# Column maxima of a gated cross-attention: TensorE's eight transposes, or block transposes on VectorE

## The chip, the cores and the metric

One core of one Trainium2 chip. The metric is the device time of one execution in microseconds (us). The engines are named as the profile names them: PE is TensorE's matmul and PEld its weight load, DVE is VectorE, ACT is ScalarE, POOL is GpSimd, SP issues the transfers.

## The reference

Eight independent batches. For each of them, x is 512 x 512 and the memory is 1601 x 256:

```python
memory_proj = einsum('bme,de->bmd', memory, W_mem)
scores = einsum('bnd,bmd->bnm', hidden_states, memory_proj) / sqrt(D)
attn = softmax(scores, axis=-1)
memory_context = einsum('bnm,bmd->bnd', attn, memory_proj)
gate = sigmoid(einsum('bnf,df->bnd', concat([hidden_states, memory_context]), W_gate) + b_gate)
fused = hidden_states + gate * memory_context
out = fused * rsqrt(mean(fused**2, -1) + 1e-6) * norm_w
```

All in fp32. The softmax runs over the 1601 rows of the memory.

## The kernel before

**Arithmetic.** Each fp32 operand of a matmul is split into a rounded high part (`..._hi`, made by ACT) and the rest (`..._lo`, made by DVE, L919), and a product is three matmuls, hi x hi, lo x hi and hi x lo (L387 to L389, L586 to L588). W_mem is moved to the other side: q = W_mem' x, scores = mem q, u = mem' p, and the context and the gate's input are products of u with W_mem and with V, the product of W_mem and the gate's second half.

**Layout.** The scores are held transposed: `s[:, t, :]` has 128 rows of the memory on the partitions (tile t of 13, the last with 65 rows) and the 512 rows of x as columns. A softmax over the memory is then one over partitions and tiles. DVE keeps a running maximum `run` (128 x 512) over the tiles (`running_max`, L931); after the last tile its 128 partitions still have to be reduced to one and the result spread over all partitions, in PSUM bank 3 (`MAX_BANK`), from where `shift` (L960) subtracts it from each tile of s. Before, this is done so: PE transposes the four 128 x 128 blocks of `run` into bank 2 (`transpose_max`, L462), DVE reduces them to `col_max` (128 x 4, L952), and PE transposes `col_max`, each column repeated 128 times, into bank 3 (`spread_max`, L474).

**Stages of a batch b.** 1. Scores: PE makes 13 tiles; ACT copies each to s, DVE takes the running maximum, splits the transposed memory (`mt_lo`) and the memory itself (`mem_lo_part`, pairs of tiles 0 to 6, after ACT's `mem_hi`). 2. PE works on what the batch before has left: the sums of its rows (L489), gate input and context of its four row tiles j (`gate_context`, `context`), while DVE does the maximum. 3. PE makes x times the gate's first half (`gate_x`, L387 to L389 with wg1t). Beside this and stage 4, DVE and ACT run the softmax in 13 steps t: `shift` of tile t+3, ACT's exponential (L755, into `p_tmp`), ACT's `p_hi`, DVE's `p_lo` of tile t; POOL adds the exponentials up (`add_p`, L1229). Among these steps stand the rest of the batch before (`gate_input` L1015, `gate_ctx` L1067, `add_x` L1075), `add_bias` (L986), and DVE's block transposes of the next batch's x and memory (L1025, L1041; a block transpose turns every 32 x 32 block in its place). 4. PE sums u over the tiles (`weighted`); it needs p_lo of each, and after tile 9 it makes q of the next batch (`query`). Then DVE makes `output` (L1084) of the batch before, splits q (`q_lo`), on which the next batch's scores wait, and u (`u_lo`).

**What sets the order.** It is written out by hand: each engine runs its instructions in the order of its own block in the code and waits on semaphores. The first batch, six batches in a loop (1 to 6) and the last one have their own variants. `SPLIT_BY_SCORES` and `SPLIT_BY_SOFTMAX` say at which step the pairs of memory tiles are split, on ACT and on DVE. The eight PSUM banks are shared by the stages.

**The waits that the prediction speaks of:** `weighted(b, t)` on p_lo of t, and for even t on `mem_lo` of its pair; `score(b+1, 0)` on `q_lo`; the last tile on copies by SP that follow p_lo of tile 12 (`stack_last_tile`); in the first batch `gate_x` 2 on `add_bias` 0; in the last batch `tail_gate` on `u_lo`.

Of the kernel before, what the change touches and what calls it, by code (L numbers as in the profile page):

```python
# [36 lines left out]
P = 128  # L37
# [6 lines left out]
def xattn_kernel(nc: bass.Bass, x, mem, w, wg, b_gate, norm_w, out):  # L44
# [19 lines left out]
    with ExitStack() as ctx:  # L64
# [54 lines left out]
        col_max = sb("col_max", [P, NT])  # L119
# [63 lines left out]
        pe_mt, pe_s, pe_max_t, pe_max_rows = sem("pe_mt"), sem("pe_s"), sem("pe_max_t"), sem("pe_max_rows")  # L183
# [42 lines left out]
        SPLIT_BY_SOFTMAX = {5: [6]}  # L226

# [154 lines left out]
        def _(pe):  # L382
# [72 lines left out]
            def transpose_max(b):  # L455


                pe.wait_ge(run_done, (MT - 1) * (b + 1))

                pe.wait_ge(s_copied, MT * (b + 1))  # L460
                for j in range(NT):
                    last = nc.tensor.transpose(  # L462
                        bank[S_BANK][:, j * P : (j + 1) * P], run[:, j * P : (j + 1) * P], ident[:, :])
                last.then_inc(pe_max_t, 1)

            def spread_max(b, first):


                pe.wait_ge(col_max_done, b + 1)
                if not first:  # L470

                    pe.wait_ge(r_done, b)
# [151 lines left out]
            def iteration(b, first, last):  # L624
                scores(b, first)
                if first:
# [6 lines left out]
                    transpose_max(b)  # L633
                    weights(V[0])
                    spread_max(b, first)
# [3 lines left out]
                else:  # L639
                    row_sums(b - 1, True)  # L640
                    gate_context(b - 1, 0)
                    transpose_max(b)
                    context(b - 1, 0)
                    gate_context(b - 1, 1)
                    spread_max(b, first)
# [271 lines left out]
        def _(dve):  # L917
# [28 lines left out]
            def reduce_max(b, first):  # L946
                if not first:

                    dve.wait_ge(pe_max_rows, b)

                dve.wait_ge(pe_max_t, b + 1)
                nc.vector.tensor_reduce(col_max[:, :], bank[S_BANK][:, :].rearrange("p (a n) -> p a n", a=NT),  # L952
                                        AX.X, ALU.max).then_inc(col_max_done, 1)

            def shift(b, t):
                if t == 0:

                    dve.wait_ge(pe_max_rows, b + 1)
# [139 lines left out]
            def iteration(b, first, last):  # L1098
                transpose_mem(b, 2)
                for p in range(MP):  # L1100
# [8 lines left out]
                    for q in SPLIT_BY_SCORES.get(p, []):  # L1109
                        mem_lo_part(b, q)  # L1110
# [18 lines left out]
                else:  # L1129
# [9 lines left out]
                    for t in range(MT):  # L1139
# [5 lines left out]
                        if t in (0, 2, 4):  # L1145
                            gate_ctx(b - 1, 1 + t // 2)
# [148 lines left out]
```

## Time and profile before

| | |
|---|---|
| median of 3 runs | 545.79 us (545.26 to 546.56) |
| the profiled execution | 546.02 us, span 544.0 us |
| granted TensorE clock | 0.998 of full speed |
| PE busy | 533.3 us, 98% |
| PEld busy | 436.6 us, 80% |
| DVE busy | 480.4 us, 88% |
| ACT busy | 315.9 us, 58% |
| POOL busy | 148.0 us, 27% |

The profiled execution takes 2.0 us more than its span, which is what lies around the first and the last instruction. A row of a timeline gives the start and the duration in us; its end is pipelined, so the next instruction of an engine may start some 0.08 us before it. A bracket at the end of a row is idle time ahead of it, with what ended it. The six batches of the loop repeat at a distance of 64.1 us; most rows below are from one of them.

### The profile page before, as it was taken

What the parts mean: (1) busy time and instruction counts of PE and PEld (TensorE: products, weight loads), DVE (VectorE), ACT (ScalarE), POOL (GpSimd) and SP (SyncE); (2) the same over time, 40 slices, a digit from 0 to 9 for tenths busy, and PEclk for the clock granted to TensorE, in tenths of its full rate; (3) what the DMA queues carried; (4) which work ended last, traced back from release to release, by engine and by line L of the source; (5) the groups of instructions that cost most, each with busy time, mean ns of one, the idle gap of its engine ahead of it and who ended that gap; (6) DMA issues with size and microseconds to landing.
All of it is one profiled execution on the core that took longest, in us unless ns stands there. A gap on an engine that the chain in (4) does not pass through costs nothing.

```text
span 544.0 us, 8854 instructions
## 1 busy us (share of the span) xinstructions
PE 533.3 (98%) x2420; PEld 436.6 (80%) x2420; DVE 480.4 (88%) x758; ACT 315.9 (58%) x601; POOL 148.0 (27%) x127
## 2 busy tenths in 40 slices
PE   8899999999999999999999999999999999999994
PEld 7776888888888888888888888888888888888883
DVE  3779958899799997999978998989979999789967
ACT  4575636566465664666465763656556575557523
POOL 0005610065002540036200660015400263004703
PEclk9999999999999999999999999999999999999999
DMA  9855363621576207841278214762068510301033
GB/s 225 262 118 92 96 107 88 113 59 41 141 159 104 93 7 170 175 107 39 85 127 171 76 39 125 161 114 72 25 159 169 120 49 30 125 30 40 1 117 116
DMA packets 185861, 56.37 MB, mean 104 GB/s; under 512 B 161756, under 2 KB 175592, under 8 KB 185844
## 3 DMA queue, kind: packets, MB, share of 16 engines
q1 hardware_dynamic: 185316, 55.64, 43.7%
q10 hardware_dynamic: 528, 0.52, 0.3%
q8 instruction: 8, 0.13, 0.1%
q14 instruction: 9, 0.07, 0.1%
HBM read 46.15 MB, written 8.39 MB: 100 GB/s over the span
## 4 chain that ended last, share of the span: by engine, by line
PE 93%; SPq 3%; DMA 2%; DVE 1%; issue 0%; ACTq 0%; POOLq 0%; POOL 0%; DVEq 0%; ACT 0%
PE bank L387 21%; PE bank L389 21%; PE bank L388 21%; PE bank L586 8%; PE bank L587 8%; PE bank L588 8%; DMA fused<-in_L_xattn_W_gate_dram 2%; SPq L262 2%; PE bank L607 1%; PE bank L489 1%; PE bank L621 1%; PE bank L462 1%; PE bank L474 1%; PE bank L570 1%; DMA x_again<-in_x_dram 1%; PE bank L569 1%
## 5 line engine op out<-in xcount | busy, mean ns | idle before, releaser
L1229 POOL TENSOR_TENSOR psum_rows<-psum_rows,p_tmp 128x512 f32<-128x512 f32 (+1 forms) x88 | 122.9, 1397 | 71.6 <-ACT p_tmp L755 70.0
L919 DVE TENSOR_TENSOR p_lo<-p_tmp,p_hi 128x512 fp32r<-128x512 f32 (+1 forms) x104 | 92.6, 891 | 5.5 <-ACT p_hi L716 5.4
L1229 POOL TENSOR_TENSOR psum_rows<-p_tmp 128x512 f32<-128x512 f32 x8 | 10.4, 1297 | 275.2 <-ACT p_tmp L755 275.2
L755 ACT ACTIVATE p_tmp<-s 128x512 f32<-128x512 f32 (+1 forms) x104 | 64.5, 626 | 30.5 <-DVE s L960 29.3
L387 PE MATMUL bank<-q_hi,mt_hi 128*128 128x512 f32 (+1 forms) x208 | 81.9, 394 | 0.0
L389 PE MATMUL bank<-q_hi,mt_lo 128*128 128x512 f32 (+1 forms) x208 | 81.3, 391 | 0.0
L388 PE MATMUL bank<-q_lo,mt_hi 128*128 128x512 f32 (+1 forms) x208 | 81.2, 390 | 0.0
L586 PE MATMUL bank<-p_hi,mem_hi 128*128 128x512 f32 (+1 forms) x196 | 76.4, 390 | 0.0
L587 PE MATMUL bank<-p_lo,mem_hi 128*128 128x512 f32 (+1 forms) x196 | 76.4, 390 | 0.0
L588 PE MATMUL bank<-p_hi,mem_lo 128*128 128x512 f32 (+1 forms) x196 | 76.3, 390 | 0.0
L716 ACT ACTIVATE s<-bank 128x512 f32<-128x512 f32 (+1 forms) x104 | 62.0, 596 | 19.5 <-PE bank L389 19.1
L960 DVE TENSOR_TENSOR s<-s,bank 128x512 f32<-128x512 f32 (+1 forms) x104 | 68.4, 671 | 0.0
L931 DVE TENSOR_TENSOR run<-run,s 128x512 f32<-128x512 f32 (+1 forms) x88 | 59.9, 681 | 8.1 <-ACT s L716 5.8
L716 ACT ACTIVATE p_hi<-p_tmp 128x512 fp32r<-128x512 f32 (+1 forms) x104 | 63.4, 616 | 0.0
L387 PE MATMUL bank<-wg1t_hi,xt_hi 128*128 128x512 f32 x128 | 50.3, 393 | 0.0
L389 PE MATMUL bank<-wg1t_hi,xt_lo 128*128 128x512 f32 x128 | 49.9, 390 | 0.0
L388 PE MATMUL bank<-wg1t_lo,xt_hi 128*128 128x512 f32 x128 | 49.8, 389 | 0.0
L774 ACT ACTIVATE gate<-gate 128x512 f32<-128x512 f32 x32 | 20.2, 633 | 49.2 <-DVE gate L1015 49.2
L919 DVE TENSOR_TENSOR mt_lo<-bank,mt_hi 128x512 fp32r<-128x512 f32 (+1 forms) x56 | 34.6, 627 | 15.9 <-ACT mt_hi L716 15.9
L716 ACT ACTIVATE mt_hi<-bank 128x512 fp32r<-128x512 f32 (+1 forms) x56 | 30.1, 550 | 29.1 <-PE bank L389 29.1
L389 PEld LDWEIGHTS bank<-q_hi,mt_lo 128*128 128x128 f32 (+1 forms) x208 | 38.2, 184 | 9.3
L388 PEld LDWEIGHTS bank<-q_lo,mt_hi 128*128 128x128 f32 (+1 forms) x208 | 38.3, 184 | 8.9
(98 smaller groups left out, 1031.0 us busy)
## 6 DMA issues: line engine op xcount, KB each, us to landing
mem_raw<-in_ctx_dram SPq DMA_DIRECT2D x48, 256.0 KB, 3.1
mem_blocks<-in_ctx_dram SPq DMA_DIRECT2D x64, 136.0 KB
x_again<-in_x_dram SPq DMA_DIRECT2D x32, 256.0 KB, 2.7
out_dram<-fused SPq DMA_DIRECT2D x32, 256.0 KB, 2.1
x_raw<-in_x_dram SPq DMA_DIRECT2D x112, 64.0 KB, 2.0
mem_blocks<-in_ctx_dram SPq DMA_DIRECT2D x56, 64.0 KB, 2.0
x_raw<-in_x_dram SPq DMA_DIRECT2D x4, 256.0 KB, 5.1
gate<-in_L_xattn_W_gate_dram SPq DMA_DIRECT2D x2, 512.0 KB, 5.6
```

Source lines behind the costliest of these rows:

```text
L387: nc.tensor.matmul(dst, a_hi, b_hi, start=(start and i == 0), stop=False)
L388: nc.tensor.matmul(dst, a_hi, b_lo, start=False, stop=False)
L389: last = nc.tensor.matmul(dst, a_lo, b_hi, start=False, stop=(stop and i == n - 1))
L586: nc.tensor.matmul(dst, mem_hi[0:r, t, cs], p_hi[0:r, t, :], start=(t == 0), stop=False)
L587: nc.tensor.matmul(dst, mem_hi[0:r, t, cs], p_lo[0:r, t % LO_RING, :], start=False, stop=False)
L588: last = nc.tensor.matmul(dst, mem_lo[0:r, t, cs], p_hi[0:r, t, :], start=False, stop=(t == MT - 1))
L716: return nc.scalar.activation(dst, src, ACT.Copy)
L755: nc.scalar.activation(p_tmp[0:r, t % TMP_RING, :], s[0:r, t, :], ACT.Exp, scale=float(D) ** -0.5).then_inc(exp_done, 1)
L919: return nc.vector.tensor_tensor(dst, src, hi.bitcast(F32), ALU.subtract)
L931: nc.vector.tensor_tensor(run[0:r, :], a, s[0:r, t, :], ALU.max).then_inc(run_done, 1)
L960: nc.vector.tensor_tensor(s[0:r, t, :], s[0:r, t, :], bank[MAX_BANK][0:r, :], ALU.subtract).then_inc(shifted, 1)
L1229: nc.gpsimd.tensor_tensor(psum_rows[0:r, :], a, p_tmp[0:r, t % TMP_RING, :], ALU.add).then_inc(p_added, 1)
```

## The change

The column maxima are made by DVE alone. It transposes the 32 x 32 blocks of `run` into bank 2, reduces each block's 32 columns to one (`col_max`, 128 x 16), takes the larger of the upper and the lower 64 partitions, then of the 32 and 32 left, copies the 32 rows to the next 32 and the 64 to the next 64, and makes a last block transpose of this (each column repeated 32 times) into bank 3. Each of these waits for the one before. PE's `transpose_max` and `spread_max` are gone. The order of DVE changes too: in the batches after the first, pairs 4 and 5 of the memory are no longer split at the end of the scores but in softmax steps 3 and 5, and pair 6 in step 6 in place of 5 (`LATE_SPLITS`); ACT's high parts stay where they were. Both first gate inputs now stand ahead of the shifts, and `gate_ctx` 0 and 1 and `add_x` 0 between the first three shifts.

```diff
+        LATE_SPLITS = {3: [4], 5: [5], 6: [6]}
...
-                for j in range(NT):
-                    last = nc.tensor.transpose(
-                        bank[S_BANK][:, j * P : (j + 1) * P], run[:, j * P : (j + 1) * P], ident[:, :])
-                last.then_inc(pe_max_t, 1)
...
-                for j in range(NT):
-                    last = nc.tensor.transpose(bank[MAX_BANK][:, j * P : (j + 1) * P],
-                                               col_max[:, j : j + 1].broadcast_to([P, P]), ident[:, :])
-                last.then_inc(pe_max_rows, 1)
...
+            def column_max(b):
+                dve.wait_ge(s_copied, MT * (b + 1))
+                dve.wait_ge(run_done, (MT - 1) * (b + 1))
+                nc.vector.transpose(blocks(bank[S_BANK][:, :]), blocks(run[:, :])).then_inc(max_blocks, 1)
+                dve.wait_ge(max_blocks, b + 1)
+                nc.vector.tensor_reduce(col_max[:, :], blocks(bank[S_BANK][:, :]), AX.X, ALU.max).then_inc(col_max_done, 1)
+                dve.wait_ge(col_max_done, b + 1)
+                nc.vector.tensor_tensor(pair_max[:, :], col_max[0 : P // 2, :], col_max[P // 2 : P, :],
+                                        ALU.max).then_inc(max_paired, 1)
+                dve.wait_ge(max_paired, b + 1)
+                nc.vector.tensor_tensor(row_max[0:BLOCK, :], pair_max[0:BLOCK, :], pair_max[BLOCK : 2 * BLOCK, :],
+                                        ALU.max).then_inc(max_joined, 1)
+                dve.wait_ge(max_joined, b + 1)
+                nc.vector.tensor_copy(row_max[BLOCK : 2 * BLOCK, :], row_max[0:BLOCK, :]).then_inc(max_doubled, 1)
+                dve.wait_ge(max_doubled, b + 1)
+                nc.vector.tensor_copy(row_max[P // 2 : P, :], row_max[0 : P // 2, :]).then_inc(max_copied, 1)
+            def spread_max(b):
+                dve.wait_ge(max_copied, b + 1)
+                nc.vector.transpose(blocks(bank[MAX_BANK][:, :]),
+                                    row_max[:, :].unsqueeze(2).broadcast_to([P, N // BLOCK, BLOCK])).then_inc(max_spread, 1)
...
-                    for q in SPLIT_BY_SCORES.get(p, []):
+                    for q in (SPLIT_BY_SCORES if p < MP - 1 or first else {}).get(p, []):
                         mem_lo_part(b, q)
...
                 else:
+                    column_max(b)
                     reciprocal(b - 1)
+                    spread_max(b)
                     gate_input(b - 1, 0)
-                    reduce_max(b, first)
+                    gate_input(b - 1, 1)
+                    shift(b, 0)
                     gate_ctx(b - 1, 0)
-                    gate_input(b - 1, 1)
+                    shift(b, 1)
+                    gate_ctx(b - 1, 1)
+                    shift(b, 2)
                     add_x(b - 1, 0)
-                    shift(b, 0)
-                    shift(b, 1)
-                    shift(b, 2)
...
-                        if t in (0, 2, 4):
+                        if t in (2, 4):
...
-                        for q in SPLIT_BY_SOFTMAX.get(t, []):
+                        for q in LATE_SPLITS.get(t, []):
```

DVE in the loop, behind the last running maximum. Before, with two splits of the memory (`mem_lo`) ahead of the reciprocal (`r_sum`) and the reduction behind the first gate input:

```order
L919 TENSOR_TENSOR mem_lo<-mem_raw,mem_hi 128x512 x2
L1007 RECIPROCAL r_sum<-bank 128x4
L1010 TENSOR_SCALAR r_half<-r_sum 128x4
L1014 ISA
L1015 SCALAR_TENSOR_TENSOR gate<-bank,r_sum,gate 128x512
L952 TENSOR_REDUCE col_max<-bank 128x4
```

Now, from the transpose of `run` to the one that fills bank 3:

```order
L931 STREAM_TRANSPOSE bank<-run 128x512
L934 TENSOR_REDUCE col_max<-bank 128x16
L937 TENSOR_TENSOR pair_max<-col_max 64x16
L941 TENSOR_TENSOR row_max<-pair_max 32x16
L945 COPY row_max<-row_max 32x16
L948 COPY row_max<-row_max 64x16
L1008 RECIPROCAL r_sum<-bank 128x4
L1011 TENSOR_SCALAR r_half<-r_sum 128x4
L953 STREAM_TRANSPOSE bank<-row_max 128x512
```

The two splits have left, the whole column maximum stands in their place, and the reciprocal has gone between its last copy and its last transpose.

DVE in the loop, a little later, up to the first `p_lo`. Before, with three shifts (`s<-s,bank`) in one piece:

```order
L1015 SCALAR_TENSOR_TENSOR gate<-bank,r_sum,gate 128x512
L1073 ISA
L1075 SCALAR_TENSOR_TENSOR fused<-fused,r_half,x_again 128x512
L960 TENSOR_TENSOR s<-s,bank 128x512 x3
L1067 SCALAR_TENSOR_TENSOR fused<-gate,bank 128x512
L960 TENSOR_TENSOR s<-s,bank 128x512
L965 REGISTER_ALU
L919 TENSOR_TENSOR p_lo<-p_tmp,p_hi 128x512
```

Now, from the second gate input on:

```order
L1016 SCALAR_TENSOR_TENSOR gate<-bank,r_sum,gate 128x512
L961 TENSOR_TENSOR s<-s,bank 128x512
L1067 REGISTER_ALU
L1068 SCALAR_TENSOR_TENSOR fused<-gate,bank 128x512
L961 TENSOR_TENSOR s<-s,bank 128x512
L1068 SCALAR_TENSOR_TENSOR fused<-gate,bank 128x512
L961 TENSOR_TENSOR s<-s,bank 128x512
L1074 ISA
L1076 SCALAR_TENSOR_TENSOR fused<-fused,r_half,x_again 128x512
L961 TENSOR_TENSOR s<-s,bank 128x512
L966 REGISTER_ALU
L897 TENSOR_TENSOR p_lo<-p_tmp,p_hi 128x512
```

The shifts are apart: `gate_ctx` 0 and 1 (`fused<-gate,bank`) and `add_x` 0 (`fused<-fused,r_half,x_again`) stand between them, and `add_x` 0, which stood ahead of all shifts, stands behind the third.

DVE in softmax steps 3 and 4 of the loop. Before, from `add_bias` 0 (`gate<-bank,bias_rows`) to `p_lo` of step 4:

```order
L986 TENSOR_TENSOR gate<-bank,bias_rows 128x512
L960 TENSOR_TENSOR s<-s,bank 128x512
L919 TENSOR_TENSOR p_lo<-p_tmp,p_hi 128x512
L982 REGISTER_ALU
L986 TENSOR_TENSOR gate<-bank,bias_rows 128x512
L1067 SCALAR_TENSOR_TENSOR fused<-gate,bank 128x512
L960 TENSOR_TENSOR s<-s,bank 128x512
L919 TENSOR_TENSOR p_lo<-p_tmp,p_hi 128x512
```

Now, from the same `add_bias` 0 to the same `p_lo`:

```order
L987 TENSOR_TENSOR gate<-bank,bias_rows 128x512
L897 TENSOR_TENSOR mem_lo<-mem_raw,mem_hi 128x512
L961 TENSOR_TENSOR s<-s,bank 128x512
L897 TENSOR_TENSOR p_lo<-p_tmp,p_hi 128x512
L983 REGISTER_ALU
L987 TENSOR_TENSOR gate<-bank,bias_rows 128x512
L1068 SCALAR_TENSOR_TENSOR fused<-gate,bank 128x512
L961 TENSOR_TENSOR s<-s,bank 128x512
L897 TENSOR_TENSOR p_lo<-p_tmp,p_hi 128x512
```

A `mem_lo` has come in between `add_bias` 0 and the shift; another stands in the same way behind `add_bias` 2 in step 5, and the short one of step 5 behind `add_bias` 3 in step 6.

PE in the loop, between the first gate input (`v_hi`) and the first context (`wt_hi`) of the batch before. Before:

```order
L387 MATMUL bank<-v_hi,u_hi 128x512
L388 MATMUL bank<-v_lo,u_hi 128x512
L389 MATMUL bank<-v_hi,u_lo 128x512
L458 REGISTER_ALU
L460 REGISTER_ALU
L462 MATMUL bank<-ident,run 128x128 x4
L387 MATMUL bank<-wt_hi,u_hi 128x512
L388 MATMUL bank<-wt_lo,u_hi 128x512
L389 MATMUL bank<-wt_hi,u_lo 128x512
```

The four transposes of `run` (L462) leave this place, and the two products follow each other; the four of `col_max` (L474) leave another like it, ahead of the second context.

## Rows read from the trace of the kernel before

**Rows 1.** The page: busy time by engine, and the chain that ended last.
```profile
PE 533.3 (98%) x2420; PEld 436.6 (80%) x2420; DVE 480.4 (88%) x758; ACT 315.9 (58%) x601; POOL 148.0 (27%) x127
...
PE 93%; SPq 3%; DMA 2%; DVE 1%; issue 0%; ACTq 0%; POOLq 0%; POOL 0%; DVEq 0%; ACT 0%
```

**Rows 2.** Groups by line and form (busy us, mean ns, idle before).
```profile
L919 DVE TENSOR_TENSOR p_lo<-p_tmp,p_hi 128x512 fp32r<-128x512 f32 x96 | 87.2, 909 | 0.0
...
L462 PE MATMUL bank<-ident,run 128*128 128x128 f32 x32 | 4.8, 272 | 0.0
```

**Rows 3.** Timeline of PE around the first four transposes (start us, us).
```profile
229.00 0.60 PE L462 MATMUL bank<-ident,run 128*128 128x128 f32 x4
229.35 0.48 PE L387 MATMUL bank<-wt_hi,u_hi 128*128 128x512 f32 x1
229.66 0.40 PE L388 MATMUL bank<-wt_lo,u_hi 128*128 128x512 f32 x1
```

**Rows 4.** Timeline of DVE, loop batch, from the last scores to the first p_lo.
```profile
228.24 1.28 DVE L919 TENSOR_TENSOR mem_lo<-mem_raw,mem_hi 128x512 fp32r<-128x512 f32 x2
229.44 0.17 DVE L1007 RECIPROCAL r_sum<-bank 128x4 f32<-128x4 f32 x1
229.65 0.17 DVE L1010 TENSOR_SCALAR r_half<-r_sum 128x4 f32<-128x4 f32 x1
...
231.32 0.69 DVE L1067 SCALAR_TENSOR_TENSOR fused<-gate,bank 128x512 f32<-128x512 f32 x1 [0.20 <-ACT gate L774]
232.40 0.75 DVE L1015 SCALAR_TENSOR_TENSOR gate<-bank,r_sum,gate 128x512 f32<-128x512 f32 x1 [0.39 <-PE bank L389]
...
236.72 0.88 DVE L919 TENSOR_TENSOR p_lo<-p_tmp,p_hi 128x512 fp32r<-128x512 f32 x1
```

**Rows 5.** Groups by line and form, DVE: the nearest to the new operations.
```profile
L1025 DVE STREAM_TRANSPOSE bank<-x_raw 128x512 f32<-128x512 f32 x28 | 19.8, 706 | 0.0
...
L952 DVE TENSOR_REDUCE col_max<-bank 128x4 f32<-128x512 f32 x8 | 5.4, 680 | 0.0
...
L919 DVE TENSOR_TENSOR mem_lo<-mem_raw,mem_hi 65x256 fp32r<-65x256 f32 x8 | 3.6, 454 | 0.0
...
L1170 DVE MEMSET ones<- 128x1 f32 x1 | 0.1, 59 | 0.8 <-PEq L1283 0.8
```

**Rows 6.** Timeline of all engines: one shift, its exponential, its add on POOL.
```profile
250.46 0.67 DVE L960 TENSOR_TENSOR s<-s,bank 128x512 f32<-128x512 f32 x1
...
251.24 0.63 ACT L755 ACTIVATE p_tmp<-s 128x512 f32<-128x512 f32 x1
...
252.03 1.30 POOL L1229 TENSOR_TENSOR psum_rows<-psum_rows,p_tmp 128x512 f32<-128x512 f32 x1 [1.88 <-ACT p_tmp L755]
```

**Rows 7.** Timeline of all engines: an add on POOL and a p_lo on DVE.
```profile
239.61 1.29 POOL L1229 TENSOR_TENSOR psum_rows<-psum_rows,p_tmp 128x512 f32<-128x512 f32 x1 [0.82 <-ACT p_tmp L755]
...
239.86 1.59 DVE L919 TENSOR_TENSOR p_lo<-p_tmp,p_hi 128x512 fp32r<-128x512 f32 x1
```

**Rows 8.** Timelines of DVE and of PEld: two results and the loads behind them.
```profile
260.06 0.66 DVE L919 TENSOR_TENSOR p_lo<-p_tmp,p_hi 128x512 fp32r<-128x512 f32 x1
...
270.68 1.28 DVE L919 TENSOR_TENSOR q_lo<-bank,q_hi 128x512 fp32r<-128x512 f32 x2
...
262.37 0.19 PEld L586 LDWEIGHTS bank<-p_hi,mem_hi 128*128 128x128 f32 x1
...
272.81 0.19 PEld L387 LDWEIGHTS bank<-q_hi,mt_hi 128*128 128x128 f32 x1
```

**Rows 9.** Timelines of DVE and of PEld, last batch.
```profile
523.97 0.69 DVE L919 TENSOR_TENSOR u_lo<-bank,u_hi 128x512 fp32r<-128x512 f32 x1
...
525.20 0.19 PEld L387 LDWEIGHTS bank<-v_hi,u_hi 128*128 128x128 f32 x1
```

**Rows 10.** Timelines of DVE and of PEld, first batch.
```profile
50.43 0.68 DVE L986 TENSOR_TENSOR gate<-bank,bias_rows 128x512 f32<-128x512 f32 x1
...
51.93 0.19 PEld L387 LDWEIGHTS bank<-wg1t_hi,xt_hi 128*128 128x128 f32 x1
```

More of the change, by code:

```diff
@@ L118, in xattn_kernel @@
         ones = sb("ones", [P, 1])
-        col_max = sb("col_max", [P, NT])
+        col_max = sb("col_max", [P, N // BLOCK])
+        pair_max = sb("pair_max", [P // 2, N // BLOCK])
+        row_max = sb("row_max", [P, N // BLOCK])
         r_sum = sb("r_sum", [P, NT])
@@ L181, in xattn_kernel @@
         pe_wt, wt_split_hi, wt_split_lo = sem("pe_wt"), sem("wt_split_hi"), sem("wt_split_lo")
-        pe_mt, pe_s, pe_max_t, pe_max_rows = sem("pe_mt"), sem("pe_s"), sem("pe_max_t"), sem("pe_max_rows")
+        pe_mt, pe_s = sem("pe_mt"), sem("pe_s")
+        max_blocks, max_paired, max_joined = sem("max_blocks"), sem("max_paired"), sem("max_joined")
+        max_doubled, max_copied, max_spread = sem("max_doubled"), sem("max_copied"), sem("max_spread")
         pe_sum, pe_ctx, pe_g, pe_gx = sem("pe_sum"), sem("pe_ctx"), sem("pe_g"), sem("pe_gx")
@@ L632, in iteration @@
                         weights(g)
-                    transpose_max(b)
                     weights(V[0])
-                    spread_max(b, first)
                     weights(V[1])
@@ L944, in mem_lo_part, with blocks @@
                 lo_part(mem_lo[0:r, ts, :], mem_raw[0:r, raw, :], mem_hi[0:r, ts, :]).then_inc(mem_has_lo, 1)
[L946 to L953, printed above, removed]
+            def blocks(ap):
+                return ap.rearrange("p (r i) -> p r i", i=BLOCK)
+            def column_max(b):
[18 more added lines that the diff above has]
+                                    row_max[:, :].unsqueeze(2).broadcast_to([P, N // BLOCK, BLOCK])).then_inc(max_spread, 1)
             def shift(b, t):
                 if t == 0:
-                    dve.wait_ge(pe_max_rows, b + 1)
+                    dve.wait_ge(max_spread, b + 1)
                 r = rows(t)
@@ L1129, in iteration @@
                 else:
+                    column_max(b)
                     reciprocal(b - 1)
+                    spread_max(b)
                     gate_input(b - 1, 0)
-                    reduce_max(b, first)
+                    gate_input(b - 1, 1)
+                    shift(b, 0)
                     gate_ctx(b - 1, 0)
-                    gate_input(b - 1, 1)
+                    shift(b, 1)
+                    gate_ctx(b - 1, 1)
+                    shift(b, 2)
                     add_x(b - 1, 0)
-                    shift(b, 0)
-                    shift(b, 1)
-                    shift(b, 2)
                     for t in range(MT):
```

9 lines of the change are left out of this document (removed).

## The prediction

> **What bounds the kernel now.** I read the page first. PE is busy for 98% of the span and makes up 93% of the chain that ended last; DVE is busy for 88% [rows 1]. So PE's order is the time, and whatever leaves it is worth its place there, as long as nobody else becomes late. Whether somebody does isn't seen in the 88%, which is a mean: DVE rests in the scores stage and hardly in the softmax stage, where its timeline shows no gap from the second gate input to the last p_lo. So I then read, for each result of DVE that PE waits for, when it is ready and when PE's weight load behind it starts. These margins decide.
>
> **What leaves PE.** Eight transposes per batch; the first four of each are 32 rows of 272 ns in all [rows 2], but pipelined. The first four begin at 229.00, the product behind them at 229.35, its second matmul at 229.66 [rows 3]. Without them the product begins at 229.00 and its second matmul one ordinary step of 0.23 later, so 0.66 - 0.23 = 0.43 goes, and I count the other four the same. That is 0.87 us per batch and 7.0 us over eight, the whole possible gain.
>
> **What comes to DVE at the maximum.** The trace has none of the new operations on this data, so they are bounded by neighbours [rows 5]. Two block transposes of 128 x 512: the one of x takes 0.71, in the order 0.63 if the next needs no result; I take 0.73 with the wait for the first and 0.63 for the last. The last reads each column 32 times in place; it could cost up to twice that; nothing in the rows gives it less, since it writes 512 columns too. The reduction takes 0.68 for 4 results; I take 0.70 for 16. Four small ones, each waiting for the last: the nearest chain is reciprocal to r_half, 229.44 to 229.65, so 0.21 each [rows 4]. The lower bound is the 59 ns of a one-column memset, the upper the 0.45 of a 65 x 256 subtraction [rows 5]. Sum: 0.10 (the chain starts behind the last running maximum, not beside it) + 0.73 + 0.70 + 4 x 0.21 + 0.63 = 3.0 us. Against it, before the first p_lo, go the two memory splits (1.20, from 228.24 to 229.44), the old reduction (0.68 less an overlap of 0.08, 0.60) and two gaps of 0.20 and 0.39, with the 0.08 of overlap that each costs [rows 4], together 2.55. The first p_lo, at 236.72, is late by 0.45 so far.
>
> **What comes into the softmax steps.** The two splits are not gone: they return in steps 3 and 5, 0.60 each. DVE has no gap there, so that is 1.20 more, 1.65 in all, before any contention.
>
> **Contention with POOL.** An add on POOL from 239.61 to 240.90 meets a p_lo that begins at 239.86; this takes 1.59 in place of 0.66 and ends 0.55 after the add does [rows 7]. Operations that read one operand from PSUM (shift, gate_input, gate_ctx, add_bias) or only one at all (the transposes) show no such length in the same places; those with two operands in SBUF do: p_lo, add_x, and the memory splits. The other way round the add ends 1.17 after the DVE operation. So it matters where each add falls. It follows its shift: shift 250.46, exponential 251.24, add 252.03 [rows 6], that is 0.78 and 0.79 (for the first add 0.78 and 0.69), if ACT is free. With these distances and DVE's steps (a duration less 0.08: 0.60 for a shift or p_lo, 0.67 for gate_input and add_x, 0.63 for a transpose) I went through the new order by hand. add_x 0 starts 1.80 after shift 1, the first add 1.47: DVE stands 0.8. add_x 1 meets the second add (0.8), p_lo 1 the third (0.6), the split of pair 4 the fourth (0.8), p_lo 3 the fifth (0.5), pair 5 the seventh (0.3), pair 6 the eighth (0.3). Sum 4.2, and each hit has some 0.3 us or more to spare. Before, p_lo takes 909 ns in the mean [rows 2] against 660 alone [rows 8], 3.0 us per batch over its 12 full tiles; in a loop batch some 0.5 of that falls behind step 6, and with 0.4 at add_x 1 the same stretch has 2.45. So 1.75 more. From step 6 on the distances are the old ones. DVE is late by 1.65 + 1.75 = 3.4 us at p_lo 6, and stays so to q_lo.
>
> The Trainium skill, SBUF — State Buffer, Who interferes with whom, says that a DVE instruction with two SBUF inputs and a GpSimd one that reads SBUF exclude each other for the whole instruction, whoever is first, and that one with a single SBUF input doesn't contend. The trace agrees in the rows named, 1.59 against 0.66 us. By the rule the late splits pay twice, as in my sum; without it they would be 549 us, the first rival.
>
> **What PE then waits for.** Before, q_lo's first half is ready at 270.68 + 0.68 = 271.36 and PE's load for the next scores starts at 272.81, a margin of 1.45, 1.40 with a signal's 0.05; p_lo 9 is ready at 260.72, its load starts at 262.37, 1.60 [rows 8]. PE comes 0.87 earlier, DVE 3.4 later: the wait is 3.4 + 0.87 - 1.40 = 2.9 per batch, most of it already taken at p_lo 6 to 9 (2.7 at the ninth). The copies behind the last p_lo, through SP, should be late by about as much and add nothing of their own. PE stands 2.9 and saves 0.87: **+2.0 us for each of six batches, +12.0**. The scores stage doesn't give it back to PE; DVE's gaps there just put it in step with PE again.
>
> **The last batch.** With no transposes of a next batch between them, p_lo 7 and p_lo 8 meet adds as well: by the same walk DVE is 4.0 late. The outputs of the batch before stand ahead of u_lo, which is ready at 523.97 + 0.69 = 524.66 for a load at 525.20 [rows 9], a margin of 0.5. 4.0 + 0.87 - 0.5 = 4.4 of waiting, net +3.5.
>
> **The first batch.** Its splits stay. DVE has 3.0 of new work against 0.60, ahead of the gate weights, 2.4; but it had 0.74 idle before the v split, and the first adds fall a little better, so add_bias 0, at 50.43, is 1.4 late. It is ready at 51.11 for a load at 51.93 [rows 10]: 1.4 + 0.87 - 0.8 = 1.5 of waiting, net +0.6. Later DVE waits for PE there, which absorbs the rest.
>
> **The sum.** 0.6 + 12.0 + 3.5 = +16.1 on 546.0, the profiled execution's own time (its span of 544.0 and 2.0 around it), makes 562.1. That execution lies 0.2 above the median of 545.8, so I say 562. The point from which it turns: up to a lateness of 0.5 in DVE the loop gains the whole 0.87, up to 1.4 it gains something.
>
> **The rivals.**
> *The adds fall no worse than before* (0.15). POOL's starts could shift in ways that my walk misses. Then DVE is late by 1.65: a wait of 1.1 and +0.25 for each loop batch (1.5), +1.5 in the last, +0.6 in the first: about +3.5, 549. For it: two or three hits rest on 0.3 of margin, and a miss of one moves all that follow. Against: two more operations with two SBUF operands stand in a stretch where POOL works half the time.
> *DVE hides it, and the time falls* (0.12). If the small operations cost near 0.06 and most adds miss, DVE is late by about 0.8 at q_lo: no wait in the loop, -0.87 six times (-5), a wait of 1.1 in the last batch (+0.2), -0.1 in the first: about 541. It decides below 1.4 us of lateness. For it: 1.4 us is a real margin, and PE, which bounds the kernel, gets shorter. Against: 1.2 of moved splits alone take nearly all of the 1.4.
> *The new operations are dear* (0.08). The small ones at 0.45 and the last transpose at twice its price add 1.0 + 0.6 = 1.6 us to DVE in every batch, and all of it is waited for: +13, 575; half of it is 568.
> *My own case* (0.65) has 555 to 568: the hits can each be off by a few tenths, and 0.8 us of lateness over eight batches is 6.4.
>
> About 0.2%, 1.1 us, is what a measurement of this kernel can tell from no change. Faster by more: 0.11. Slower by more: all of my case, the dear one and nearly all of the first rival, 0.84. The same: 0.05. The range is 547 to 568; below it lies the hiding case, above it half of the dear one.
>
> **What would show it.** Right: PE with waits, on p_lo in `weighted` at tiles 6 to 9 and on q_lo or the copies at the end of a batch, together near 2.9 us per loop batch; a batch every 66.1 us in place of 64.1; seven new DVE operations in 3.0 us; POOL's first add begun just ahead of add_x 0, and splits of the memory with 0.9 to 1.5 us in steps 3 and 5; p_lo 6 later by 3.4 against the last running maximum. Wrong: PE without waits at a step of 63.3 us (the hiding case), waits of about 1 us (the first rival), or waits of PE on something that I hold to be early, as the gated context before `context` 2, whose margin I put at only 0.1.

## The result, and the profile after

The changed kernel takes 561.14 us in the median of 4 runs (560.70 to 562.44), the kernel before 545.63 on the same chip: a ratio of 1.0285, 95% interval 1.0264 to 1.0305. The profiled execution took 562.44, with a span of 560.6 against 544.0, 16.6 more.

The page of the kernel after, busy time and the chain that ended last, which answers to [rows 1], and the granted clock in 40 slices:

```profile
PE 537.9 (96%) x2356; PEld 429.1 (77%) x2356; DVE 507.5 (91%) x806; ACT 318.8 (57%) x601; POOL 146.9 (26%) x127
...
PEclk9999999999999999999999999999999999999978
...
PE 50%; DVE 33%; issue 10%; SPq 3%; DMA 2%; ACT 1%; DVEq 1%; POOL 0%; ACTq 0%; POOLq 0%
```

PE's share of the chain has fallen from 93% to 50% and DVE's has risen from 1% to 33%, though DVE's busy share rose only from 88% to 91%. The 537.9 of PE are more than the 533.3 of before, with 64 matmuls fewer. In the last stretch, which has the two slices of lower clock, PE is busy for 55.9 us in place of 52.5. In a loop batch it reads busy for 64.4 of 65.8 in place of 64.1 of 64.1, because the modelled end of a matmul (0.39 long, 0.23 apart) covers part of a wait behind it: PE's idle time understates what it waits.

The last running maximum of each batch cuts the span into eight stretches. Before, in batch 1, in the batch that most rows are from, and in the last:

```profile
99.41 0.69 DVE L931 TENSOR_TENSOR run<-run,s 65x512 f32<-65x512 f32 x1
...
227.63 0.69 DVE L931 TENSOR_TENSOR run<-run,s 65x512 f32<-65x512 f32 x1
...
483.99 0.69 DVE L931 TENSOR_TENSOR run<-run,s 65x512 f32<-65x512 f32 x1
```

After:

```profile
100.11 0.69 DVE L909 TENSOR_TENSOR run<-run,s 65x512 f32<-65x512 f32 x1
...
231.74 0.69 DVE L909 TENSOR_TENSOR run<-run,s 65x512 f32<-65x512 f32 x1
...
494.91 0.69 DVE L909 TENSOR_TENSOR run<-run,s 65x512 f32<-65x512 f32 x1
```

The first stretch is 0.7 longer, each of the six of the loop 1.70 ((494.91 - 100.11)/6 = 65.80 in place of 64.10; 10.2 in all), and what follows 483.99 and 494.91 is 5.7 longer (60.0 before, 65.7 after). The sum is the 16.6.

DVE in the loop batch that begins in that second row, up to q_lo:

```profile
232.46 0.73 DVE L931 STREAM_TRANSPOSE bank<-run 128x512 f32<-128x512 f32 x1
233.22 0.69 DVE L934 TENSOR_REDUCE col_max<-bank 128x16 f32<-128x512 f32 x1
233.95 0.17 DVE L937 TENSOR_TENSOR pair_max<-col_max 64x16 f32<-64x16 f32 x1
234.15 0.16 DVE L941 TENSOR_TENSOR row_max<-pair_max 32x16 f32<-32x16 f32 x1
...
234.55 0.17 DVE L948 COPY row_max<-row_max 64x16 f32<-64x16 f32 x1
...
235.04 0.72 DVE L953 STREAM_TRANSPOSE bank<-row_max 128x512 f32<-128x512 f32 x1
235.67 1.37 DVE L1016 SCALAR_TENSOR_TENSOR gate<-bank,r_sum,gate 128x512 f32<-128x512 f32 x2
...
239.94 1.48 DVE L1076 SCALAR_TENSOR_TENSOR fused<-fused,r_half,x_again 128x512 f32<-128x512 f32 x1
...
243.20 1.50 DVE L1076 SCALAR_TENSOR_TENSOR fused<-fused,r_half,x_again 128x512 f32<-128x512 f32 x1
...
245.22 1.24 DVE L897 TENSOR_TENSOR p_lo<-p_tmp,p_hi 128x512 fp32r<-128x512 f32 x1
...
249.44 1.49 DVE L897 TENSOR_TENSOR mem_lo<-mem_raw,mem_hi 128x512 fp32r<-128x512 f32 x1
...
251.45 1.18 DVE L897 TENSOR_TENSOR p_lo<-p_tmp,p_hi 128x512 fp32r<-128x512 f32 x1
...
256.17 1.00 DVE L897 TENSOR_TENSOR mem_lo<-mem_raw,mem_hi 128x512 fp32r<-128x512 f32 x1
...
259.52 0.74 DVE L897 TENSOR_TENSOR mem_lo<-mem_raw,mem_hi 65x256 fp32r<-65x256 f32 x1
...
278.00 1.29 DVE L897 TENSOR_TENSOR q_lo<-bank,q_hi 128x512 fp32r<-128x512 f32 x2
```

Each small operation starts 0.20 after the last. The column maximum runs from 232.46 to 235.67, 3.21 with the two reciprocal operations in it. `add_x` 0 takes 1.48 and the split of pair 4 takes 1.49, where alone they take 0.70 to 0.75 and 0.67: POOL had begun just ahead of them, as its own timeline shows:

```profile
239.57 1.29 POOL L1233 TENSOR_TENSOR psum_rows<-p_tmp 128x512 f32<-128x512 f32 x1 [30.32 <-ACT p_tmp L733]
...
249.08 3.00 POOL L1233 TENSOR_TENSOR psum_rows<-psum_rows,p_tmp 128x512 f32<-128x512 f32 x2 [3.17 <-ACT p_tmp L733]
```

q_lo starts 46.26 behind the last running maximum (278.00 - 231.74). Before it was 43.05 (227.63 to the 270.68 of [rows 8]): DVE is 3.21 later. PE's weight loads of the same batch, those with a wait:

```profile
262.17 0.19 PEld L568 LDWEIGHTS bank<-p_hi,mem_hi 128*128 128x128 f32 x1 [0.75 <-issue]
263.90 0.19 PEld L568 LDWEIGHTS bank<-p_hi,mem_hi 128*128 128x128 f32 x1 [0.50 <-DVE p_lo L897]
265.76 0.19 PEld L568 LDWEIGHTS bank<-p_hi,mem_hi 128*128 128x128 f32 x1 [0.64 <-issue]
268.10 0.19 PEld L568 LDWEIGHTS bank<-p_hi,mem_hi 128*128 128x128 f32 x1 [1.11 <-DVE p_lo L897]
...
278.74 0.19 PEld L392 LDWEIGHTS bank<-q_hi,mt_hi 128*128 128x128 f32 x1 [0.34 <-DVE q_lo L897]
```

Four stand in `weighted`, at p_lo 6 to 9, and one small one at q_lo. Those put down to "issue" begin right behind a p_lo too (one starts at 261.38 and ends at 262.05, the load follows at 262.17). The brackets add up to 3.3 us; before, the load behind q_lo ran 0.24 ahead of its matmul (272.81 and 273.05), so the brackets are an upper bound of what PE loses.

### The profile page after: what moved, and what is told of

Read it like the earlier page. It is cut to its first block, busy times and chain, and to the rows that moved or that the text cites. A ratio compares the mean times of both kernels' runs of the same rounds, so it can differ in the third digit from the quotient of the medians.

```text
span 560.6 us, 8759 instructions
## 1 busy us (share of the span) xinstructions
PE 537.9 (96%) x2356; PEld 429.1 (77%) x2356; DVE 507.5 (91%) x806; ACT 318.8 (57%) x601; POOL 146.9 (26%) x127
## 4 chain that ended last, share of the span: by engine, by line
PE 50%; DVE 33%; issue 10%; SPq 3%; DMA 2%; ACT 1%; DVEq 1%; POOL 0%; ACTq 0%; POOLq 0%
PE bank L392 14%; PE bank L394 13%; PE bank L393 13%; DVE p_lo L897 8%; DVE s L961 8%; DVE fused L1068 3%; DVE gate L987 3%; DVE bank L1026 3%; PE bank L568 3%; PE bank L569 3%; PE bank L570 3%; DVE gate L1016 2%; SPq L267 2%; DMA fused<-in_L_xattn_W_gate_dram 2%; DVE xt_lo L897 1%
## 5 line engine op out<-in xcount | busy, mean ns | idle before, releaser
L897 DVE TENSOR_TENSOR p_lo<-p_tmp,p_hi 128x512 fp32r<-128x512 f32 (+1 forms) x104 | 86.1, 829 | 5.5 <-ACT p_hi L694 5.4
L568 PE MATMUL bank<-p_hi,mem_hi 128*128 128x512 f32 (+1 forms) x196 | 79.2, 404 | 9.0 <-DVE p_lo L897 8.2
L961 DVE TENSOR_TENSOR s<-s,bank 128x512 f32<-128x512 f32 (+1 forms) x104 | 69.7, 673 | 0.0
L568 PEld LDWEIGHTS bank<-p_hi,mem_hi 128*128 128x128 f32 (+1 forms) x196 | 36.7, 187 | 27.7 <-DVE p_lo L897 10.8
L897 DVE TENSOR_TENSOR mem_lo<-mem_raw,mem_hi 128x512 fp32r<-128x512 f32 (+1 forms) x56 | 47.1, 842 | 0.9 <-ACT mem_hi L694 0.9
```

The costliest lines, as they stand in the source:

```text
L568: nc.tensor.matmul(dst, mem_hi[0:r, t, cs], p_hi[0:r, t, :], start=(t == 0), stop=False)
L897: return nc.vector.tensor_tensor(dst, src, hi.bitcast(F32), ALU.subtract)
L961: nc.vector.tensor_tensor(s[0:r, t, :], s[0:r, t, :], bank[MAX_BANK][0:r, :], ALU.subtract).then_inc(shifted, 1)
```

## The experiments

Every ratio is to the kernel before, timed beside it on the same chip. "Period" is the distance of the last running maxima in the loop.

**1. Without POOL's traffic** (`e1_short_adds`). The changed kernel with POOL's adds of the exponentials over 1 of 512 columns; the row sums of the other 511 columns are left out.

```diff
-                nc.gpsimd.tensor_tensor(psum_rows[0:r, :], a, p_tmp[0:r, t % TMP_RING, :], ALU.add).then_inc(p_added, 1)
+                nc.gpsimd.tensor_tensor(psum_rows[0:r, 0:1], a, p_tmp[0:r, t % TMP_RING, 0:1], ALU.add).then_inc(p_added, 1)
...
+            nc.gpsimd.memset(psum_rows[:, :], 1.0)
```

The operand `a` is cut to one column in the same way.

> The changed kernel, but POOL's adds of the exponentials cover one column of 512 (its sums of rows, and so the output, are not the reference's). My theory (VectorE is late in the softmax steps, half of it by contention with POOL): all hits go, those of before too. VectorE is then late by 0.45 + 1.2 - 2.45 - 0.5 = -1.3 us at q_lo, PE waits for nothing in the loop and keeps the 0.87 per batch of the dropped transposes: 538 to 540 us, a batch every 63.3 us. Rival (the added VectorE work is what counts, POOL does not): 555 us or more.

Measured: 538.87, ratio 0.988 (0.986 to 0.990), period 63.15 ((477.13 - 98.26)/6). p_lo, and POOL's adds:

```profile
L897 DVE TENSOR_TENSOR p_lo<-p_tmp,p_hi 128x512 fp32r<-128x512 f32 x96 | 64.7, 675 | 0.3 <-ACT p_hi L694 0.2
...
L1233 POOL TENSOR_TENSOR psum_rows<-psum_rows,p_tmp 128x1 f32<-128x1 f32 x80 | 26.4, 330 | 149.6 <-ACT p_tmp L733 149.5
```

With all of DVE's new work and all of its new order in place, the kernel is faster than before by the whole of the eight transposes: 64.10 - 63.15 = 0.95 per batch. This doesn't show that the new work fits into the margin of 1.4 by itself, for the collisions that the kernel before had are gone too: q_lo starts 41.67 behind the last running maximum, 1.4 earlier than before, while the first p_lo, at 9.46, is still 0.37 late. It shows that without collisions nothing is left to wait for in the loop.

**2. The late splits alone** (`e2_late_splits_alone`). The kernel before, TensorE's transposes kept, with one part of the new order.

```diff
+        LATE_SPLITS = {3: [4], 5: [5], 6: [6]}
...
-                    for q in SPLIT_BY_SCORES.get(p, []):
+                    for q in (SPLIT_BY_SCORES if p < MP - 1 or first else {}).get(p, []):
...
-                        for q in SPLIT_BY_SOFTMAX.get(t, []):
+                        for q in LATE_SPLITS.get(t, []):
```

> The kernel before with one part of the change alone: memory pairs 4, 5 and 6 are split in softmax steps 3, 5 and 6; PE keeps its eight transposes and the maximum is the old one. My theory: 1.2 us more in the steps and about 1.1 more contention, less a margin of 1.4 at q_lo, is 0.9 us per loop batch and up to 2 in the last: about 553 us. Rival (the splits' place is harmless, the new maximum is the cause): 546 us.

Measured: 554.08, ratio 1.0145 (1.0109 to 1.0181), period 64.88. PE still has its eight transposes, so the 0.78 per batch is waiting alone, and DVE has no operation more than before. Its timeline in the loop, behind a last running maximum at 229.54:

```profile
233.23 0.69 DVE L1068 SCALAR_TENSOR_TENSOR fused<-gate,bank 128x512 f32<-128x512 f32 x1 [0.77 <-PE bank L390]
...
238.63 0.90 DVE L920 TENSOR_TENSOR p_lo<-p_tmp,p_hi 128x512 fp32r<-128x512 f32 x1
...
246.35 1.48 DVE L920 TENSOR_TENSOR mem_lo<-mem_raw,mem_hi 128x512 fp32r<-128x512 f32 x1
```

The first p_lo stands 9.09 behind the maximum (238.63 - 229.54), and before it is 9.09 too (227.63 to the 236.72 of [rows 4]). So the 1.20 us that left this place gave DVE nothing: it now waits for PE there, 0.58 ahead of the first gate input, where there was no wait, and 0.77 in the row shown, where it was 0.20. Where the splits came in there is no such wait, and they meet the adds besides, 1.48 in place of 0.67. q_lo starts 2.32 later than before (45.37 behind the maximum, 43.05 before), against a margin of 1.4.

**3. The new maximum alone** (`e3_maximum_alone`). The changed kernel with the order and the splits of before; the maximum stands where the reduction stood.

```diff
-                    for q in (SPLIT_BY_SCORES if p < MP - 1 or first else {}).get(p, []):
+                    for q in SPLIT_BY_SCORES.get(p, []):
...
+                    reciprocal(b - 1)
+                    gate_input(b - 1, 0)
                     column_max(b)
-                    reciprocal(b - 1)
                     spread_max(b)
-                    gate_input(b - 1, 0)
+                    gate_ctx(b - 1, 0)
                     gate_input(b - 1, 1)
-                    shift(b, 0)
-                    gate_ctx(b - 1, 0)
-                    shift(b, 1)
-                    gate_ctx(b - 1, 1)
-                    shift(b, 2)
                     add_x(b - 1, 0)
+                    shift(b, 0)
+                    shift(b, 1)
+                    shift(b, 2)
...
-                        if t in (2, 4):
+                        if t in (0, 2, 4):
...
-                        for q in LATE_SPLITS.get(t, []):
+                        for q in SPLIT_BY_SOFTMAX.get(t, []):
```

> The new column maximum with VectorE's order otherwise as before: splits early, both gate inputs, gate_ctx and add_x as they were. My theory: VectorE late by 1.65 us at q_lo with no new hits by POOL, a wait of 1.1 less 0.87 per loop batch, 1.5 in the last (about 2.5 more if PE's clock falls in its wait there): 549 us, up to 552. Rival (the new maximum makes the loss): 559 to 561 us.

Measured: 549.13, ratio 1.0059 (1.0039 to 1.0080), period 64.32. The waits of the weight loads:

```profile
PEld bank L392 <- DVE fused L1068: 7.6, 8, 1.1
...
PEld bank L392 <- DVE q_lo L897: 1.9, 6, 0.4
```

The size is as expected, the place isn't. PE stands once per batch at `context` 3, whose bank has to be free of `gate_ctx` 1: 

```profile
238.14 0.68 DVE L1068 SCALAR_TENSOR_TENSOR fused<-gate,bank 128x512 f32<-128x512 f32 x1
...
238.88 0.19 PEld L392 LDWEIGHTS bank<-wt_hi,u_hi 128*128 128x128 f32 x1 [1.02 <-DVE fused L1068]
```

In the order of before `gate_ctx` 1 stands behind the first three shifts, and the new maximum makes it 1.7 us later against the last running maximum (238.14 - 228.57 = 9.57; before 235.52 - 227.63 = 7.89). In the changed order it stands ahead of the third shift, and no load waits for it. Whether that gains time these runs don't show, since it is q_lo that sets the period here too: it starts 44.71 behind the maximum, 1.66 later than before, 0.2 more than the margin of 1.45 in [rows 8], and the load behind it still waits.

**4. The last transpose twice** (`e4_spread_twice`), to price one more microsecond of DVE ahead of the softmax.

```diff
                 dve.wait_ge(max_copied, b + 1)
+                nc.vector.transpose(blocks(bank[MAX_BANK][:, :]),
+                                    row_max[:, :].unsqueeze(2).broadcast_to([P, N // BLOCK, BLOCK])).then_inc(max_once, 1)
+                dve.wait_ge(max_once, b + 1)
                 nc.vector.transpose(blocks(bank[MAX_BANK][:, :]),
```

> The changed kernel with its last block transpose made twice, one after the other: 0.75 us more on VectorE in each of eight batches. My theory: VectorE's lateness is waited for in full, 8 x 0.75 = 6 us more than the changed kernel: 567 us. Rival (PE's waits come from elsewhere, as the copies through SP or the loads): under 563 us.

Measured: 567.05, ratio 1.0397 (1.0376 to 1.0419), period 66.54, 0.74 over the changed kernel's for an operation of 0.73. All margin is spent: what DVE gets ahead of the softmax is paid in full. Part of it is paid at once, at `context` 2:

```profile
PEld bank L393 <- DVE fused L1073: 4.3, 7, 0.6
```

**5. The splits behind p_lo** (`e5_splits_behind_p_lo`). The same steps, but each split stands behind the step's p_lo. By my walk (the prediction's way of going through DVE's order step by step) one of the three, pair 5, would miss the adds there, and the short one would meet one in full.

```diff
-                        for q in LATE_SPLITS.get(t, []):
-                            mem_lo_part(b, q)
                         softmax(b, t, not last)
+                        for q in LATE_SPLITS.get(t, []):
+                            mem_lo_part(b, q)
```

> The changed kernel with the three late memory splits of steps 3, 5 and 6 made right behind that step's p_lo, no longer ahead of its shift. A walk like that of the prediction: pair 4 now meets POOL's fifth add, which starts at once behind the fourth and is held up by p_lo 3, and loses as much as it and p_lo 3 lost before; pair 5 is free (0.3 less), the short pair 6 meets the ninth add (0.8 more). So no gain: 561 to 563 us. Rival (a split is free behind p_lo, since an add starts 1.57 us behind its shift and two operations fit): 1.5 less per batch, about 552 us.

Measured: 564.71, ratio 1.0323 (1.0290 to 1.0356), period 66.68. The splits came out as walked:

```profile
252.96 1.78 DVE L897 TENSOR_TENSOR mem_lo<-mem_raw,mem_hi 128x512 fp32r<-128x512 f32 x1
...
259.47 0.67 DVE L897 TENSOR_TENSOR mem_lo<-mem_raw,mem_hi 128x512 fp32r<-128x512 f32 x1
...
263.07 1.51 DVE L897 TENSOR_TENSOR mem_lo<-mem_raw,mem_hi 65x256 fp32r<-65x256 f32 x1
...
267.52 0.95 DVE L897 TENSOR_TENSOR p_lo<-p_tmp,p_hi 128x512 fp32r<-128x512 f32 x1
...
271.40 1.37 DVE L897 TENSOR_TENSOR p_lo<-p_tmp,p_hi 128x512 fp32r<-128x512 f32 x1
```

A split of 65 x 256 that takes 0.41 alone took 1.51. I had stopped the walk at p_lo 6, and behind it p_lo 8 and p_lo 10 are longer than in the changed kernel (0.65 and 1.18 there). That is 0.5 per batch. The walk's own terms, 0.8 more for the short pair and 0.3 less for pair 5, make another 0.5, which is 3 us over six batches and not the "no gain" that I made of it. Together they are the 0.9 by which q_lo is later than in the changed kernel (47.17 behind the maximum against 46.26) and the period longer. The time is 1.7 above the upper end of what I expected, and the loop alone costs 5.3; the last stretch gives 2.9 of it back (62.83 in place of 65.69), where u_lo's load comes 1.8 earlier and the slow clock described below is shorter. A walk has to go on to the result that is waited for.

**6. u_lo ahead of the outputs in the last batch** (`e6_u_lo_ahead_in_the_last`).

```diff
+                    if last:
+                        u_lo_part(b, 0)
                     dve.wait_ge(root_done, b)
                     for j in range(NT):
                         output(b - 1, j)
...
-                for c in range(CT):
+                for c in range(1 if last else 0, CT):
                     u_lo_part(b, c)
```

> The changed kernel with one edit in the last batch alone: u_lo's first half ahead of the four outputs of the batch before, so that PE doesn't stand 2 us ahead of the tail. In the changed kernel's profile PE's granted clock reads 0.50 for some 6 us behind that wait and the 13 matmuls there take 0.43 instead of 0.23 us each, 2.6 us in all. If the wait brings the clock down: about 1.5 less of waiting and 2.6 less of slow clock, 557 us, with the clock at 1.00 there. Rival (the clock falls for another reason at that point, as the load of the stores): 1.5 less at most, 559.5 us, clock still 0.50.

Measured: 558.22, ratio 1.0206 (1.0180 to 1.0233), 0.8% or 4 us below the changed kernel by the ratios, and 4.1 by the profiled spans (556.5 against 560.6). Moving one operation of 0.6 us takes away a wait of 2.0 and leaves one of 0.7, on u_lo's second half. The rest is the clock. Mean granted clock (third from the end of a row) and busy times in the tail of the changed kernel:

```profile
535.00:539.00 4.00, 2.56 (x16) 1.92 (x14) 3.22 (x5) 1.19 (x2) 0.74 (x1) 0.90 0.40 151
539.00:545.00 6.00, 5.83 (x14) 4.57 (x15) 1.28 (x5) 0.00 (x0) 0.00 (x0) 0.50 0.50 162
```

and in the same stretches here:

```profile
535.00:539.00 4.00, 4.00 (x23) 3.44 (x22) 3.17 (x5) 1.20 (x2) 0.62 (x1) 1.00 0.24 89
539.00:545.00 6.00, 5.69 (x26) 4.39 (x25) 5.16 (x11) 2.48 (x5) 0.41 (x1) 1.00 0.64 213
```

**7. An order laid around the adds** (`e7_around_the_adds`). The changed kernel, its new maximum kept, with `add_x` 0 and 1 and the three late splits put where the walk finds POOL at rest; two of the four outputs moved behind q_lo.

```diff
-        LATE_SPLITS = {3: [4], 5: [5], 6: [6]}
+        LATE_SPLITS = {5: [4], 8: [5], 11: [6]}
...
                     shift(b, 1)
+                    add_x(b - 1, 0)
                     gate_ctx(b - 1, 1)
                     shift(b, 2)
-                    add_x(b - 1, 0)
...
-                        if t in ADD_AT:
+                        if t in ADD_AT[1:]:
                             add_x(b - 1, ADD_AT.index(t) + 1)
-                        for q in LATE_SPLITS.get(t, []):
-                            mem_lo_part(b, q)
                         softmax(b, t, not last)
+                        if t == ADD_AT[0]:
+                            add_x(b - 1, 1)
+                        for q in LATE_SPLITS.get(t, []):
+                            mem_lo_part(b, q)
...
-                    for j in range(NT):
+                    for j in range(2):
                         output(b - 1, j)
+                    if last:
+                        u_lo_part(b, 0)
```

In the first batch `add_bias` also goes ahead of the step's shift and p_lo.

> The changed kernel with VectorE's order laid around POOL's adds by the same walk: add_x 0 behind the second shift and add_x 1 behind p_lo 1, pairs 4, 5, 6 split behind p_lo in steps 5, 8 and 11, two of the outputs behind q_lo, u_lo's first half behind two outputs in the last batch, add_bias ahead of shift and p_lo in the first. By the walk VectorE is then early by 0.3 us at p_lo 9 and PE waits for nothing: the 0.87 per batch is kept, 539 to 540 us, a batch every 63.3 us, faster than both. Rival (VectorE's added 3 us can't be hidden by order, since it is busy throughout): 548 us or more.

Measured: 539.40, ratio 0.9871 (0.9846 to 0.9895), faster than before and after, period 63.15 ((477.92 - 99.05)/6). add_x 0 and the three splits, each alone:

```profile
232.38 0.75 DVE L1076 SCALAR_TENSOR_TENSOR fused<-fused,r_half,x_again 128x512 f32<-128x512 f32 x1
...
247.93 0.67 DVE L897 TENSOR_TENSOR mem_lo<-mem_raw,mem_hi 128x512 fp32r<-128x512 f32 x1
...
255.12 0.67 DVE L897 TENSOR_TENSOR mem_lo<-mem_raw,mem_hi 128x512 fp32r<-128x512 f32 x1
...
261.68 0.41 DVE L897 TENSOR_TENSOR mem_lo<-mem_raw,mem_hi 65x256 fp32r<-65x256 f32 x1
```

DVE does the same operations as in the changed kernel in 484.3 us of busy time in place of 507.5, and the period is that of the run without POOL's traffic. The p_lo that met an add before still do (0.91, 1.38 and 1.19 in steps 3, 4 and 10). q_lo starts 41.78 behind the maximum, 1.27 earlier than before, and that is the two outputs that now stand behind it; with them ahead it would start about where it did before, which the margin allows (an estimate from the rows, not run). The waits at p_lo 6 to 9 stand ahead of the outputs, so that it is the order that removed them: p_lo 9 starts 32.15 behind the maximum, against 32.43 before and 35.64 in the changed kernel.

**8. The same order without the new maximum** (`e8_order_without_the_maximum`). The kernel before, its eight transposes kept, with the edits of experiment 7; the head of the softmax is then:

```diff
                     reciprocal(b - 1)
                     gate_input(b - 1, 0)
                     reduce_max(b, first)
-                    gate_ctx(b - 1, 0)
                     gate_input(b - 1, 1)
-                    add_x(b - 1, 0)
                     shift(b, 0)
+                    gate_ctx(b - 1, 0)
                     shift(b, 1)
+                    add_x(b - 1, 0)
+                    gate_ctx(b - 1, 1)
                     shift(b, 2)
```

> The kernel before with the order of e7_around_the_adds (the splits of pairs 4 to 6 behind p_lo of steps 5, 8 and 11, add_x 0 and 1 and gate_ctx 0 and 1 in e7's places, add_bias ahead in the first batch, two of the four outputs behind q_lo, u_lo 0 between them in the last batch); the maximum stays with TensorE's eight transposes. Theory: the time is PE's order as long as DVE isn't late, before already had a margin of 1.4 us at q_lo and no waits on DVE in the loop, so a better order of DVE has nothing to give it: 545 to 546.5, ratio 1.000, a loop period of 64.1; e7's gain of 6.5 is then the eight transposes alone, which it puts at 0.81 each batch. Rival: a good part of e7's gain is its order, which before could have had as well: 542 or less, with a period under 63.6. Other rival: reduce_max is behind the gate input and PE's second four transposes wait for it, so that the new order costs something here: 547 or more, with a wait of PE on col_max.

Measured: 546.71 (10 runs), ratio 1.0016 (0.9999 to 1.0033), period 64.10 ((485.45 - 100.86)/6). The only wait of the weight loads on DVE, besides one of 0.3 on q_lo:

```profile
PEld bank L587 <- DVE p_lo L920: 1.1, 1, 1.1
```

The loop is exactly that of before: an order that makes DVE earlier gives nothing to a kernel whose PE doesn't wait. The first batch got longer by 1.45 (100.86 against 99.41), where the place of `add_bias` is the only edit that applies and one p_lo is waited for; that part of the order is a loss, and with it the median lies 0.2 above the range expected. So the 0.95 per batch of experiment 7 is the eight transposes, and the order is what lets PE have it.

## Why the prediction was right, and where its sizes were off

The time, 561.14, was forecast as 562, and the mechanism is the one named. By its steps:

- *What leaves PE.* Put at 0.87 per batch, it is 0.95 (experiments 1 and 7). From the first gate input's product to the third's, PE takes 6.50 before (227.53 to 234.03) and 5.55 after (231.63 to 237.18). I had counted the transposes and the pipeline behind them, 2 x 0.43; the other 0.1 is that the matmuls behind them are 0.24 apart in place of 0.23.
- *The maximum on DVE.* Put at 3.0, it is 3.2 with the reciprocal's two operations, which stand in it and delay the last transpose by 0.3 (235.04 in place of 234.75, one step behind the last copy), and starts 0.12 late; 3.0 without them. The small operations are 0.20 apart against the 0.21 taken, the transposes take 0.73 and 0.72, the reduction 0.69. The dear rival is refuted.
- *Contention.* All seven hits that were walked are there. Over what each takes alone, `add_x` 0 and 1 take some 0.8 each, p_lo 1 0.6, pair 4 0.8, p_lo 3 0.5, pair 5 and the short pair 0.3 each, 4.1 in all against 4.2. DVE is late by 3.2, not 3.4, at q_lo. One step of the working doesn't follow as it stands: 3.0 less 0.5 plus 0.4 isn't 2.45. The 3.0 is a mean over all eight batches; the p_lo of the loop batch itself lose 2.6, and with that the 2.45 holds. The Trainium skill, SBUF — State Buffer, Who interferes with whom, has a VectorE instruction with two SBUF inputs contend with a GpSimd one that reads SBUF, and calls the port they share an exclusive lock. The rows agree: such an operation takes 1.48 and 1.49 us behind a begun add and 0.67 to 0.75 beside none. That the collisions with POOL decide is shown from both sides: without the traffic (experiment 1), and with it but with `add_x` and the splits laid beside it (experiment 7), the period is 63.15 and not 65.80. They aren't all of the lateness: the new maximum without any new hit makes q_lo 1.66 late (experiment 3). The first rival, in which the adds fall no worse than before, is refuted.
- *What PE waits for.* Forecast 2.9 per batch and net +2.0; it waits 1.70 + 0.95 = 2.65, net +1.70. The net doesn't depend on the size of the transposes, for what PE saves it waits; it is DVE's lateness less the margin. The lateness is 0.2 smaller (the first p_lo is 1.10 late, where 0.45 and 0.8 were worked out), and the margin is 1.5 in place of 1.4. It had been read between weight loads. The load behind q_lo is 1.82 later against the maximum (278.74 - 231.74 in place of 272.81 - 227.63), but the second matmul of the scores only 1.68 (279.08 - 231.74 in place of 273.29 - 227.63), since before the load ran ahead of its matmul and now both start together. The waits stand at tiles 6 to 9 and at q_lo, as forecast, and nothing waits at `context` 2, where the margin was put at 0.1: the gated context is ready at 238.23, the load is at 238.31. Experiment 4 shows that an operation of 0.73 more on DVE makes it wait 0.6 there.
- *The first batch.* Forecast +0.6, measured +0.7; the load on `add_bias` 0 waits 1.75.
- *The last batch.* Forecast +3.5, measured +5.7. DVE is 3.5 late at u_lo (538.43 - 494.91 = 43.52, before 39.98), not 4.0. The tail's first load is at 539.17, 44.26 behind the last running maximum, against 41.21 before (the 525.20 of [rows 9] less 483.99): 3.05. What the sum lacked is the other 2.6, PE at half its clock behind that wait (below). The loop, 1.8 below its forecast of 12, and the tail, 2.2 above, nearly cancel, so that the total is closer than its terms.
- *The rival in which the time falls* had the right condition: DVE late by less than 1.4 us at q_lo. Its price of 541 didn't follow from its 0.8 of lateness: above 0.5 a part of the 0.87 is waited for, so that it should have been some 542.5. No run has DVE late by 0.8. In experiments 1 and 7 it is early at q_lo (by 1.4 and 1.3), and in experiment 1 the loop gains 0.95 six times (5.7), and the first and the last stretch gain 1.15 and 0.94.

Experiments 2 and 3 have one part each and show +0.78 and +0.22 per batch, together 1.0 and not 1.70, because each alone has the margin to spend. The latenesses at q_lo don't add up either: 2.32 and 1.66, against 3.21 in the changed kernel. In experiment 2 the 1.20 that left the place ahead of the softmax is lost in waits for PE; in the changed kernel the new maximum fills it. In all three the period is longer by the lateness less some 1.5. Parts that spend the same margin can't be priced one by one.

## What to carry to other kernels

When work is moved from the engine that sets the time to one that follows it closely, price the move by the margin at the next result that is waited for, and walk the new order down to that result with the other engines' starts in it. Operations of VectorE with two SBUF operands took up to 2.7 times as long as alone (1.78 for 0.67 us in experiment 5), a short one 3.7 times (1.51 for 0.41), when they met an add of GpSimd, so their place is worth more than their number: the same 806 DVE instructions make this kernel 2.9% slower or 1.3% faster than before. And an order that suits the follower is worth nothing until the leader has been shortened, nor the shortening without the order; try them together.

## What the runs showed of the hardware that was not expected

Behind the wait of 2.0 us on u_lo, PE ran at half its clock. The timeline of the changed kernel:

```profile
539.17 0.79 PE L392 MATMUL bank<-v_hi,u_hi 128*128 128x512 f32 x1 [1.61 <-DVE u_lo L897]
539.76 0.63 PE L393 MATMUL bank<-v_lo,u_hi 128*128 128x512 f32 x1
...
544.45 0.63 PE L392 MATMUL bank<-v_hi,u_hi 128*128 128x512 f32 x1
544.88 0.47 PE L393 MATMUL bank<-v_lo,u_hi 128*128 128x512 f32 x1
```

From 539.76 to 544.88 matmuls are 0.43 apart, from 545.19 on 0.23 again; 13 steps of 0.20 more are the 2.6 us. The granted clock of that stretch is 0.50, the lower of the two levels (1.2 GHz), and 1.00 behind it. The 0.90 over the 4 us before it means, with two levels, that the clock fell some 0.8 us before the load, within the wait (an estimate). The stretch before the fall had PE waiting for p_lo several times, and then for u_lo. The same fall stands behind the wait on u_lo in experiment 2 (2.04 long, clock 0.57 from 533 to 537), in experiment 5 (2.04 long, clock 0.50 from 544 to 546) and in experiment 3:

```profile
528.00:532.00 4.00, 4.00 (x11) 3.16 (x12) 0.93 (x3) 0.00 (x0) 0.00 (x0) 0.57 0.69 224
```

There the wait was only 1.10, and PE had not waited for p_lo by more than 0.2 ahead of it. But in the profile of experiment 4 the clock stayed at 1.00 behind a wait of 2.04 at the same place, and it never fell in the loop, whose waits are of up to 1.1 but scattered, nor behind the 1.75 of the first batch. What decides it these runs don't settle; where the wait on u_lo was cut to 0.73 or to nothing (experiments 6 and 7), it fell only after PE's last matmul. The mean clock accounts for a part of the difference between runs at most: of the changed kernel, the slowest has 562.44 at 0.989 and the fastest 560.70 at 0.995, but another has 561.17 at 0.989.

The other way round, the add on POOL is held up too: the two adds that start at 249.08 take 3.00 together, beside the 2.6 of two alone, and DVE's blocked operation ends some 0.55 us behind the add that blocks it.
